# Residual rows added by VectorE at the seam, picks behind the first projection, remainder products last

## The reference

```python
res = x
h = layer_norm(x, ln1_scale, ln1_offset)
x = res + cross_attention(h, ctx, wq1, ..., bias_k1, bias_v1)     # 16 heads of 128, 1500 keys + 1 bias key
res = x
h = layer_norm(x, ln2_scale, ln2_offset)
x = res + cross_attention(h, ctx, wq2, ..., bias_k2, bias_v2)
h = layer_norm(x, ln_mlp_scale, ln_mlp_offset)
x = x + gelu(h @ w_fc1 + b_fc1) @ w_fc2 + b_fc2                   # 256 -> 1024 -> 256
```

## Time and profile before

| | |
|---|---|
| Median of 3 executions | 1191.36 us (1190.72 to 1191.61) |
| The profiled execution's own time | 1191.98 us |
| Its span in the profile | 1190.2 us |
| TensorE busy | 1178.3 us, 99% of the span |
| VectorE, ScalarE, GpSimd busy | 893.2, 770.4, 870.5 us |
| TensorE clock | nine tenths of full speed or more in all 40 slices |

### The profile page before, as it was taken

The page is one execution under the profiler, slowest core; times in us unless marked ns, Lnnn a source line. Parts: engine busy times, 40 slices in busy tenths (PEclk is TensorE's granted clock), DMA queues, the critical chain, the costliest instruction groups (busy, mean ns, idle before and its releaser), DMA issues.

```text
span 1190.2 us, 26498 instructions
## 1 busy us (share of the span) xinstructions
PE 1178.3 (99%) x7664; PEld 1098.7 (92%) x7664; DVE 893.2 (75%) x1654; ACT 770.4 (65%) x1514; POOL 870.5 (73%) x741
## 2 busy tenths in 40 slices
PE   8999999999999999999999999999999999999999
PEld 7788999999999999998998999999999999999898
DVE  6888768686867687777786877777777777777854
ACT  6756666666666666676685666666666666667766
POOL 4659778787878788677552878787969696967772
PEclk9999999999999999999999999999999999999999
DMA  5311222222222222233330122222222222222331
GB/s 166 114 56 53 64 73 62 73 61 73 60 74 59 75 59 75 48 72 94 96 98 19 40 63 74 61 75 58 75 58 74 60 74 60 72 50 72 71 102 44
DMA packets 148299, 83.62 MB, mean 70 GB/s; under 512 B 121181, under 2 KB 122605, under 8 KB 148249
## 3 DMA queue, kind: packets, MB, share of 16 engines
q1 hardware_dynamic: 147560, 82.23, 26.8%
q10 hardware_dynamic: 688, 0.80, 0.2%
HBM read 68.56 MB, written 0.53 MB: 58 GB/s over the span
## 4 chain that ended last, share of the span: by engine, by line
PE 95%; DVE 2%; ACT 1%; issue 1%; DMA 1%; DVEq 0%; SPq 0%; ACTq 0%
PE psum L808 39%; PE psum L815 14%; PE psum L821 14%; PE psum L816 13%; PE psum L773 6%; PE psum L861 5%; PE psum L787 3%; PE psum L721 1%; DVE g_prod L1354 1%; PE psum L737 0%; DVE oth L1597 0%; PE psum L842 0%; ACT oth L1202 0%; PE psum L760 0%; DVE t_max L1463 0%
## 5 line engine op out<-in xcount | busy, mean ns | idle before, releaser
L628 POOL TENSOR_TENSOR pt<-slots,pt 125x512 fp32r<-125x512 f32 (+3 forms) x384 | 454.2, 1191 | 155.4 <-ACT slots L1125 149.4
L808 PE MATMUL psum<-qs,ctx 128*125 128x384 f32 (+1 forms) x2304 | 527.5, 367 | 0.4 <-ACT slots L1144 0.4
L808 PEld LDWEIGHTS psum<-qs,ctx 128*125 128x125 f32 x2304 | 397.2, 186 | 40.4 <-ACT slots L1144 1.0
L815 PE MATMUL psum<-ctx,pt 125*128 125x258 f32 (+1 forms) x1344 | 378.5, 283 | 0.7 <-ACT on L1132 0.6
L816 PE MATMUL psum<-ctx,pt 125*128 125x256 f32 (+1 forms) x1344 | 376.9, 282 | 0.0
L821 PE MATMUL psum<-ctx,pt 125*128 125x258 f32 (+1 forms) x1344 | 369.4, 282 | 0.0
L1122 ACT ACTIVATE pt<-slots 125x512 fp32r<-125x512 f32 (+3 forms) x384 | 221.5, 577 | 220.6 <-DVE slots L1447 216.5
L1463 DVE TENSOR_TENSOR t_max<-psum,t_max 125x512 f32<-125x512 f32 (+1 forms) x282 | 175.4, 622 | 152.6 <-PE psum L808 150.6
L815 PEld LDWEIGHTS psum<-ctx,pt 125*128 125x128 f32 (+1 forms) x1344 | 253.5, 189 | 12.9 <-ACT on L1132 2.5
L816 PEld LDWEIGHTS psum<-ctx,pt 125*128 125x128 f32 (+1 forms) x1344 | 254.2, 189 | 6.5
L821 PEld LDWEIGHTS psum<-ctx,pt 125*128 125x128 f32 (+1 forms) x1344 | 250.5, 190 | 0.3 <-POOL pt L628 0.2
(11 more groups left out here) (115 smaller groups left out, 1032.9 us busy)
## 6 DMA issues: line engine op xcount, KB each, us to landing
tr_stage<-ctx_tr SPq DMA_DIRECT2D x60, 375.0 KB, 3.2
nat_stage<-ctx_nat SPq DMA_DIRECT2D x60, 375.0 KB
w_raw<-weights SPq DMA_DIRECT2D x70, 256.0 KB, 2.7
qt<-turn SPq DMA_DIRECT2D x256, 32.0 KB, 2.0
qt<-turn SPq DMA_DIRECT2D x224, 24.0 KB, 1.9
dk_rest<-dk_rows SPq DMA_DIRECT2D x6, 256.0 KB, 3.9
w_raw<-weights ACTq DMA_DIRECT2D x2, 256.0 KB, 4.8
dk_first<-dk_rows SPq DMA_DIRECT2D x2, 256.0 KB, 3.4
```

What stands on the lines that cost most here:

```text
L628: nc.gpsimd.tensor_tensor(split_weights(h, LO, c), logits(h, c), as_f32(split_weights(h, HI, c)), ALU.subtract).then_inc(pt_lo, 1)
L808: last = mm(scores(h, k, first), ctx_tr_chunk(half, a, c), qs[h][:, m, half, 0:R], start=(half, a, m) == terms[0], stop=(half, a, m) == te ...
L815: mm(out_bank[:, 0:D + 2], hi, ctx_nat_hi(c), start=(c == 0), stop=False, skip_group_check=True)
```

## The change

Three things change in each of the two layers:

1. `residual` is taken out. The first head's output product starts the banks (`start=True`), and at the end of the layer VectorE adds each row group: `row_sums` writes `xres = Y_BANK + xres`, waits for its own result, and the statistics and the normalisation read `xres`. ScalarE's copies back and all waits for them (`saved`) go.
2. The 16 pick products move from ahead of the first projection to between the projections of head 0 and head 1.
3. Where `project` reads contexts, its order becomes HI x HI, LO weights x HI, HI weights x LO: the product with the contexts' remainder comes last instead of second.

```diff
--- before.py
+++ after.py
@@ -753,17 +753,12 @@
                         if c == DC - 1:
                             last.then_inc(done, 1)
 
-            def residual(m):
-
-                pe.wait_ge(xb_ready, INIT + m * RG + RG)
-                for g in range(RG):
-                    mm(Y_BANK[g][0:RGP, 0:D], ident[0:RGP, 0:RGP], xres[:, g, :], start=True, stop=False)
-
             def project(out_bank, u, job, moving, ready, more):
 
 
                 pe.wait_ge(w_hi, INIT + job + 1)
-                for a, m in TERMS:
+                order = TERMS if ready is None else (TERMS[0], TERMS[2], TERMS[1])
+                for a, m in order:
                     if (a, m) == (LO, HI):
                         pe.wait_ge(w_lo, INIT + job + 1)
                     elif ready is not None:
@@ -771,7 +766,7 @@
                         pe.wait_ge(counter, value)
                     for c in range(DC):
                         last = mm(out_bank, w[u][:, a, c * P:(c + 1) * P], moving(m, c),
-                                  start=(a, m, c) == (HI, HI, 0), stop=(not more and (a, m, c) == (LO, HI, DC - 1)))
+                                  start=(a, m, c) == (HI, HI, 0), stop=(not more and (a, m, c) == (*order[-1], DC - 1)))
                 return last
 
             def queries(u, n, job):
@@ -843,12 +838,14 @@
                 else:
                     project(C_BANK[u][:, 0:ROWS], u, job, lambda m, c: ht[:, m, c, :], None, False).then_inc(c_mm, 1)
 
-            def first_contexts(n, job):
+            def first_contexts(n, job, picks):
 
                 for u in range(2):
                     pe.wait_ge(c_lo, INIT + n + u - 3)
                     project(C_BANK[u][:, 0:ROWS], u, job + u, lambda m, c, u=u: oth[u][:, m, c, :],
                             ((oth_hi, INIT + n + u + 1), (oth_lo, INIT + n + u + 1)), True).then_inc(oth_used, 1)
+                    if u == 0:
+                        picks()
                 pe.wait_ge(p80_lo, INIT + n // H + 1)
                 for u in range(2):
                     pe.wait_ge(dvm_ready, INIT + n + u + 1)
@@ -892,7 +889,7 @@
                 for u in range(4):
                     if not (last_quad and u >= 2):
                         head_context((u + 2) % 4, n + (u + 2), job + (u + 2), extra)
-                        output_rows(u, n + u, first and u == 0 and not extra)
+                        output_rows(u, n + u, first and u == 0)
                 if last_quad:
                     last_output_rows(n + 2)
 
@@ -923,7 +920,6 @@
                         carried_queries(u, l * H + quad * 4 + u)
 
                 first_blocks(l, l * JOBS, Q_BANK, q_mm)
-                pe.wait_ge(saved, INIT + l * RG)
                 query_quad(0, True, False)
                 with pe.Fori(1, QUADS - 1) as quad:
                     query_quad(quad, False, False)
@@ -988,22 +984,24 @@
                 batch_steps(B, False, True)
                 pe.wait_ge(on_act, INIT + (l + 1) * (2 * GROUPS) - 2)
                 pe.wait_ge(on_dve, INIT + (l + 1) * (3 * B) - 1)
-                residual(l)
                 pe.wait_ge(on_act, INIT + (l + 1) * (2 * GROUPS) - 1)
                 pe.wait_ge(on_dve, INIT + (l + 1) * (3 * B))
                 context_transposes(0, 2, OT_BANK)
                 pe.wait_ge(on_act, INIT + (l + 1) * (2 * GROUPS))
                 context_transposes(2, GT[1], OT_LAST)
 
-                pe.wait_ge(consts_in, 16 * N_CONSTS)
-                pe.wait_ge(pn_ready, INIT + (l + 1) * GROUPS)
-                settle(pe)
-                for j in range(TQ):
-                    last = mm(PICK_BANK[0:EXTRA, j * NT:(j + 1) * NT], pick[:, j, :], pn_extra[:],
-                              start=(j == 0), stop=True, skip_group_check=True)
-                last.then_inc(pn_picked, 1)
+                def picks():
+
+                    pe.wait_ge(consts_in, 16 * N_CONSTS)
+                    pe.wait_ge(pn_ready, INIT + (l + 1) * GROUPS)
+                    settle(pe)
+                    for j in range(TQ):
+                        last = mm(PICK_BANK[0:EXTRA, j * NT:(j + 1) * NT], pick[:, j, :], pn_extra[:],
+                                  start=(j == 0), stop=True, skip_group_check=True)
+                    last.then_inc(pn_picked, 1)
+
                 heads, jobs = l * H, l * JOBS + H
-                first_contexts(heads, jobs)
+                first_contexts(heads, jobs, picks)
                 output_quad(heads, jobs, True, True, False)
                 with pe.Fori(1, QUADS - 1) as quad:
                     output_quad(heads + quad * 4, jobs + quad * 4, True, False, False)
@@ -1037,7 +1035,7 @@
 
                 act.wait_ge(ln_chain, INIT + m * LN_CHAIN + LN_CHAIN)
                 for g in range(1, RG, 2):
-                    go(xn[:, g, :], Y_BANK[g][0:RGP, 0:D] if m else xres[:, g, :], ACT.Identity,
+                    go(xn[:, g, :], xres[:, g, :], ACT.Identity,
                        bias=ln_b[:, g:g + 1], scale=ln_r[:, g:g + 1]).then_inc(xn_act, 1)
 
             def norm(m):
@@ -1233,9 +1231,6 @@
                 if l + 1 == LAYERS:
                     weight_hi(LAYERS * JOBS + 3, 3, LAYERS * 8)
                 norm(l + 1)
-                act.wait_ge(xn_dve, INIT + (l + 2) * (RG // 2))
-                for g in range(RG):
-                    go(xres[:, g, :], Y_BANK[g][0:RGP, 0:D], ACT.Copy).then_inc(saved, 1)
 
             def gelu(f):
                 n = LAYERS * H + f
@@ -1256,12 +1251,13 @@
         def _(dve):
             V = nc.vector
 
-            def rows_of(m, g):
-
-                return Y_BANK[g][0:RGP, 0:D] if m else xres[:, g, :]
-
             def statistics(m, g):
-                V.bn_stats(ln_stat[:, g, :], rows_of(m, g)).then_inc(ln_stats, 1)
+                V.bn_stats(ln_stat[:, g, :], xres[:, g, :]).then_inc(ln_stats, 1)
+
+            def row_sums(m, g):
+
+                V.tensor_tensor(xres[:, g, :], Y_BANK[g][0:RGP, 0:D], xres[:, g, :], ALU.add).then_inc(row_sum, 1)
+                dve.wait_ge(row_sum, INIT + (m - 1) * RG + g + 1)
 
             def aggregate(m, g):
 
@@ -1284,7 +1280,7 @@
                 dve.wait_ge(ln_chain, INIT + base + 4)
                 V.scalar_tensor_tensor(ln_b[:], ln_mv[:, :, 0], -1.0, ln_r[:], ALU.mult, ALU.mult).then_inc(ln_chain, 1)
                 for g in range(0, RG, 2):
-                    V.tensor_scalar(xn[:, g, :], rows_of(m, g), ln_mv[:, g, 0:1], ln_r[:, g:g + 1],
+                    V.tensor_scalar(xn[:, g, :], xres[:, g, :], ln_mv[:, g, 0:1], ln_r[:, g:g + 1],
                                     ALU.subtract, ALU.mult).then_inc(xn_dve, 1)
                 while_waiting()
                 if m == 0:
@@ -1305,7 +1301,8 @@
             def add_bias(m):
 
                 dve.wait_ge(bo_in, m * 16 + 16)
-                dve.wait_ge(saved, INIT + m * RG)
+                dve.wait_ge(row_sum, INIT + m * RG)
+                dve.wait_ge(xn_act, INIT + (m + 1) * (RG // 2))
                 for g in range(RG):
                     V.tensor_tensor(xres[:, g, :], xres[:, g, :], bo[:], ALU.add).then_inc(xb_ready, 1)
 
@@ -1330,8 +1327,10 @@
 
             def output_statistics(m, jobs):
 
+                dve.wait_ge(xb_ready, INIT + m * RG)
                 for g in range(RG):
                     rows_complete(m - 1, jobs, g)
+                    row_sums(m, g)
                     statistics(m, g)
                     if g > 0:
                         aggregate(m, g - 1)
```

More of the change, by code:

```diff
@@ L264, in build @@
         c_mm, c_hi, c_lo, g32_ready = sem("c_mm"), sem("c_hi"), sem("c_lo"), sem("g32_ready")
-        y_mm, xb_ready, saved, x_ready = sem("y_mm"), sem("xb_ready"), sem("saved"), sem("x_ready")
+        y_mm, xb_ready, row_sum, x_ready = sem("y_mm"), sem("xb_ready"), sem("row_sum"), sem("x_ready")
         out_written = sem("out_written")
@@ L277, in build @@
             "pe": [w_used, xt_mm, q_mm, qp_mm, lb_mm, s_mm, pv_mm, ot_mm, pn_picked, oth_used, c_mm, y_mm],
-            "act": [saved, ln_root, xn_act, w_hi, h_hi, q_hi, qp_out, most_qs_hi, first_qs_hi, copied, exp_hi, exp_done, on_act, ot_out,
+            "act": [ln_root, xn_act, w_hi, h_hi, q_hi, qp_out, most_qs_hi, first_qs_hi, copied, exp_hi, exp_done, on_act, ot_out,
                     p80_hi, oth_early, oth_hi, c_hi, g32_ready],
-            "dve": [filled, x_ready, ln_stats, ln_aggr, ln_chain, xn_dve, h32_ready, h_lo, dk_ready, cq_step, cq_ready,
+            "dve": [row_sum, filled, x_ready, ln_stats, ln_aggr, ln_chain, xn_dve, h32_ready, h_lo, dk_ready, cq_step, cq_ready,
                     dv_ready, gp_ready, g_split, q_lo, first_qs_lo, lb_rows_ready, nat_hi, tr_hi, max_done,
```

## The result

The changed kernel takes 1198.96 us, the median of 6 runs (1196.96 to 1199.48), against 1191.43 us for the kernel before in the same session (1190.72 to 1192.07, 6 runs). The ratio is 1.0060 with a 95% interval of 1.0050 to 1.0069: slower by 7.5 us, where 2.4 was forecast and 1195.4 was the range's end. Among the runs further down, one of the first experiment (2333.59 us) and one of the fourth (6562.76 us) stand far outside all others at a full clock; the ratios leave them out, the medians hold them and move by 0.2 us at most.

What follows compares the result with a forecast made beforehand. TensorE was taken to bound the kernel (95% of the chain). Two seams at +0.1 and two norms at +1.15 us make 2.5, taken as 2.4: 1191.36 + 2.4 = 1193.8 us, range 1190.5 to 1195.4.

Steps and rivals of the forecast that it cites:

- The waits: After attention, TensorE waits ahead of the context transposes (0.8 us) and ahead of the first projection (1.6 us).
- 0.7 was forecast: After attention in each layer, the first output rows start at 545.2 against 544.49, 0.7 us late.
- The wait for head 2's remainder: At head 2's projection, TensorE waits about 0.7 us for DVE's remainder of the contexts.
- gain of 0.1: At the MLP, the first Gelu may come 0.1 us sooner without ScalarE's copies before it.
- part 2's list: From first projection to first output rows: steps timed with 448-column products at 0.203 us, ending 0.7 us late.
- the forecast's rivals: Seams give back all, 1189.1 us, 12%; half, 1192.4, 20%; POOL holds statistics, 1195.1, 12%; weight waits everywhere, 1196.6, 3%.
- I take all 0.6 back: Between first and third output row blocks, the 0.6 us wait for head 4's remainder disappears.
- no wait in either order: At the heads behind head 4, neither product order makes TensorE wait: no cost.
- up to 0.3: At head 5, late ACT and POOL may make the weights' remainder cost up to 0.3 us.
- not +0.1: Each seam, the stretch after attention, costs +0.7 - 0.6 = +0.1 us; bounds -0.5 and +0.5.
- the norm: At each layer norm, VectorE's added sums cost net +1.15 us; bounds 0.9 and 1.8.
- TensorE's slack: At each layer norm, slack before TensorE's later transposes takes 0.15 us off the cost.

Runs made afterwards that it cites:

- the first experiment: The changed kernel with 8 fillers ahead of the context transposes and 11 behind them: 1197.59 us, ratio 1.0052.
- the fourth: Pick move and new product order on the kernel before, identity products kept: 1194.29 us, ratio 1.0023.
- fillers that fit: The changed kernel with 3 fillers ahead of the context transposes and 5 behind them: 1194.51 us, ratio 1.0030.
- part 1 with fillers: The kernel before with residual rows added by VectorE, ScalarE's copies out, and 8 fillers in the identity products' place: 1192.97 us, ratio 1.0013.
- part 3 alone: The kernel before with only the contexts' remainder product moved last, for all heads: 1191.04 us, ratio 0.9997.
- heads 2 and 4 reordered: The kernel before with the contexts' remainder product last for heads 2 and 4 only: 1190.95 us, ratio 0.9997.
- picks back: The changed kernel with the picks ahead of the first projection again: 1195.16 us, ratio 1.0035.
- part 1 alone: The kernel before with residual rows added by VectorE and ScalarE's copies out, picks and product order as before: 1195.23 us, ratio 1.0036.

## Why the prediction was wrong, step by step

**What held.** TensorE sets the end. The waits came at the forecast places and near the forecast sizes (0.8 and 1.6 forecast, 1.02 and 1.41 measured; the forecast's own times give 0.97 for the first, 536.42 less 535.45, and its 0.8 is how much sooner the transposes end), since the `pn_extra` copy again stands 1.27 us behind POOL. With the clock kept up, the first output rows come 9.62 us behind the reciprocal instead of 8.81: 0.8 late, 0.7 was forecast. The wait for head 2's remainder, given as a sign at about 0.7, is 0.36 in that run and absent at the changed kernel's first seam, where ACT comes later still; so the 0.7 is right as a sum and not in this piece. No gain of 0.1 shows at the MLP: from the first products behind the last norm to the end of the span it is 24.8 us in both.

**The step that failed: part 2's list, "products of 448 columns at 0.203 us".** It carried the pace of the old seam into a new one and summed the waits as time lost alone. The waits also lower the clock, and the products behind them then took up to twice as long. Of the forecast's rivals none had this, and it carries the time out of the range: with the clock kept up by fillers the changed kernel takes 1194.51 us, inside it. In the profiled execution the clock is 1.9 + 0.9 us (changed kernel against fillers that fit). With the clock out of the way the parts add up: part 1 with fillers gives 50.61 (-0.05), part 3 alone 50.51 (-0.15), parts 2 and 3 51.77 (so +1.26 for part 2), and 50.66 - 0.05 - 0.15 + 1.26 = 51.72, where the changed kernel with fitting fillers has 51.76. Part 2 was not run alone.

**The second failed step: part 3, "I take all 0.6 back" and "no wait in either order" for the heads behind.** 0.6 was forecast between the first and the third block of output rows. 0.42 of it comes back (second period 3.02 instead of 3.44 between starts of output rows; the 0.43 ahead of the first stands in part 2's list). Then the third period is 3.55 instead of 2.87: 0.7 us go to POOL's mask product (in the changed kernel it starts at 554.26, 0.09 behind DVE's remainder, and takes 1.26 us). It was bounded at "up to 0.3", as a wait for weights; it is another product of POOL, and the cause is which of DVE and POOL starts first: with the mask product moved ahead of the split the third period is 2.87 again and the seam 0.65 shorter. At full clock the seam is thus +1.1 (0.8, less 0.4, plus 0.7) and not +0.1.

**A mis-sized term: the norm.** 1.15 forecast, 1.28 measured. Up to the last statistics it is +1.26 from the fillers' start, where +1.25 was forecast. Behind them it is +0.02, where +0.05 for ScalarE and -0.15 for TensorE's slack made -0.10: most of the slack was not there.

**The sum.** Forecast 2.4. In the profiled pair: 2.7 the clock, 2 x 1.1 the order, 2 x 1.28 the norms, less 0.1 and less 0.7 of luck ahead of the first seam: 6.7 of span, and 0.7 around it, 7.4. That the medians differ by nearly the same, 7.5, does not show that they are made up in the same way. The prediction read the Trainium skill ("VectorE: DVE Perf Modes", "The DRAIN you can't avoid") as leaving no overlap, which would have given 1.4 a norm. That section itself says that an operation that is not held starts earlier, and the trace agrees: the second sum starts at 587.87, 0.34 us behind the statistics at 587.53 that take 0.43.

**What stays open.** The five other runs of the changed kernel have a mean clock of 0.999 against the profiled run's 0.995, so less time at the low level, and spans of 1194.8 to 1196.5, only 0.4 to 2.1 less than the 1196.9. A mean of 0.999 is at most 3.6 us at the low level, which can cost 1.8 us of work; yet these five spans are 2.1 to 3.8 us above the 1192.7 that is the middle one with fitting fillers. So the 2.7 us of the clock are measured for the profiled execution alone, and part of the others' excess is not explained; some of it can be what varies ahead of the first seam. How the falls were spread over their seams isn't shown. Nor was it tried how short a wait would leave the clock alone.

## What to carry to other kernels

Work on TensorE that is no use to the result, or could be done elsewhere, may be what fills a wait: take it out on paper together with the wait that then shows, and price the products behind that wait at the low clock as well, since here two waits of 1.0 and 1.4 us cost 0.9 to 1.9 us a seam on top in slow products. Before moving work from an engine with cover (identity products in a wait) to the engine that is on the path (VectorE ahead of the norm), ask what covers it there: nothing did, and each norm grew by 1.28 us for four additions of 0.39 to 0.42. And where VectorE and GpSimd work side by side, a shift of some tenths of a us decides which goes first (the mask product started 0.33 us ahead of DVE before, 0.10 behind it with heads 2 and 4 reordered): look for the GpSimd product that is needed next and put it first.

## What the runs showed that was not expected

The clock can be lost at the middle of a kernel with little standing still: with 1.02 us of waiting, six transposes and 0.66 us of waiting (part 1 alone) it fell to 0.50 for 3.4 us in both layers of the profiled run, when the next products already ran. A single wait of 0.98 us behind full work (parts 2 and 3) did not lower it.

The time around the span goes with it. In all runs of kernels whose clock stayed at 1.00 it is 1.7 to 1.9 us (over 50 runs, those of the kernel before among them). In the changed kernel's six it is 2.2 to 3.0, and with picks back and with part 1 alone 1.7 to 3.1 from run to run. That is up to 1.3 us that no row of the span shows, and 0.7 us of the difference in the profiled pair. Its cause was not found.
